# Four graph layers on one core: the identity of pass 3 added into the adjacency tiles, and the normalization's scale and bias made on GpSimd

## What is computed

```python
h = relu(layernorm(x)); x = x + (D_r^-1 A) h W_in + (D_c^-1 A^T) h W_out
h = relu(layernorm(x)); x = x + silu(A silu(A h W + b) W + b)
h = relu(layernorm(x)); x = x + relu((A_n h) W + b)        # A_n = s (A + I) s, s = rsqrt(rowsum(A + I))
h = relu(layernorm(x)); x = x + relu(A_n (h W) + b)        # the same A_n
```

## Time and profile before

| | before |
| --- | --- |
| median of 3 runs | 1132.54 us (1132.07 to 1133.21) |
| profiled execution | 1133.05 us |
| its span, first to last instruction | 1131.3 us |
| TensorE, busy share of the span | 98% |
| VectorE | 93% |
| ScalarE | 81% |
| GpSimd | 4% |
| granted TensorE clock | 0.999 (2.4 GHz) |
| HBM | 360 GB/s over the span |

### The profile page before, as it was taken

How to read it: one execution, slowest core, us unless ns; L and a number is a source line. 1 busy time by engine, 2 the same in 40 slices (tenths; PEclk the granted TensorE clock), 3 DMA queues, 4 the chain that set the end, 5 groups by cost and what they waited for, 6 DMA issues and landing times.

```text
span 1131.3 us, 14740 instructions
## 1 busy us (share of the span) xinstructions
PE 1107.9 (98%) x5056; PEld 912.8 (81%) x5056; DVE 1049.6 (93%) x1452; ACT 912.9 (81%) x1278; POOL 48.0 (4%) x40
## 2 busy tenths in 40 slices
PE   5999999999999999999999999999999999999998
PEld 4778888888888778888888888888888888788886
DVE  6899997999999999898988999999999999998987
ACT  6999987799788578788887888888778778877774
POOL 0000000000000000000000111112111121100000
PEclk9999999999999999999999999999999999999999
DMA  9999998999998899999999999999999999999992
GB/s 328 404 391 393 405 409 313 341 393 409 371 377 315 308 381 375 409 371 360 376 373 383 332 371 364 345 374 340 393 348 347 368 361 335 337 410 370 380 365 113
DMA packets 113835, 408.36 MB, mean 361 GB/s; under 512 B 12640, under 2 KB 13920, under 8 KB 113760
## 3 DMA queue, kind: packets, MB, share of 16 engines
q1 hardware_dynamic: 113760, 407.42, 95.3%
HBM read 405.27 MB, written 2.10 MB: 360 GB/s over the span
## 4 chain that ended last, share of the span: by engine, by line
PE 72%; DVE 17%; ACT 3%; issue 3%; DMA 3%; SPq 1%; ACTq 0%; DVEq 0%
PE bank L701 45%; PE bank L705 23%; DVE a_lo L485 11%; PE bank L722 3%; DMA raw<-in_adj_t_dram 2%; ACT a_hi L357 1%; DVE x_sb L580 1%; ACT a_hi L359 1%; DMA raw<-in_adj_dram 1%; DVE stats L516 1%; DVE acc L573 1%; DVE h_lo L485 1%; SPq L299 1%; DVE h_lo L509 1%; PE bank L763 0%
## 5 line engine op out<-in xcount | busy, mean ns | idle before, releaser
L485 DVE TENSOR_TENSOR a_lo<-raw,a_hi 128x1024 fp32r<-128x1024 f32 x560 | 659.2, 1218 | 40.7 <-ACT a_hi L357 21.9
L701 PE MATMUL bank<-a_hi,h_hi 128*128 128x512 f32 x1400 | 437.2, 393 | 12.1 <-DVE h_lo L509 10.3
L705 PE MATMUL bank<-a_lo,h_hi 128*128 128x512 f32 x1400 | 434.9, 392 | 5.6 <-DVE a_lo L485 4.8
L357 ACT ACTIVATE a_hi<-raw 128x1024 fp32r<-128x1024 f32 x368 | 376.9, 1055 | 71.0 <-PE bank L705 55.6
L701 PE MATMUL bank<-a_hi,h_lo 128*128 128x512 f32 x1400 | 432.0, 390 | 0.0
L705 PEld LDWEIGHTS bank<-a_lo,h_hi 128*128 128x128 f32 x1400 | 260.8, 188 | 70.0 <-DVE a_lo L485 17.1
L701 PEld LDWEIGHTS bank<-a_hi,h_hi 128*128 128x128 f32 x1400 | 259.1, 188 | 65.1 <-DVE h_lo L509 10.2
L701 PEld LDWEIGHTS bank<-a_hi,h_lo 128*128 128x128 f32 x1400 | 263.1, 188 | 55.6
L359 ACT ACTIVATE a_hi<-raw 128x1024 fp32r<-128x1024 f32 x192 | 201.8, 1054 | 27.0 <-PE bank L705 12.7
L485 DVE TENSOR_TENSOR a_lo<-acc,a_hi 128x1024 fp32r<-128x1024 f32 x144 | 170.5, 1219 | 14.3 <-ACT a_hi L357 11.6
L357 ACT ACTIVATE a_hi<-acc 128x1024 fp32r<-128x1024 f32 x144 | 148.4, 1055 | 24.9 <-PE bank L705 23.8
(11 more groups left out here) (75 smaller groups left out, 420.8 us busy)
## 6 DMA issues: line engine op xcount, KB each, us to landing
raw<-in_adj_t_dram SPq DMA_DIRECT2D x496, 512.0 KB, 6.7
acc<-in_adj_t_dram SPq DMA_DIRECT2D x144, 512.0 KB, 6.5
raw<-in_adj_dram SPq DMA_DIRECT2D x128, 512.0 KB, 7.0
out_dram<-x_sb SPq DMA_DIRECT2D x7, 256.0 KB, 6.7
x_sb<-in_x_dram SPq DMA_DIRECT2D x3, 512.0 KB, 11.8
x_sb<-in_x_dram SPq DMA_DIRECT2D x2, 256.0 KB, 4.1
out_dram<-x_sb SPq DMA_DIRECT2D x2, 128.0 KB, 1.7
w_sb<-in_L_gnn_W_dram SPq DMA_DIRECT2D x3, 64.0 KB, 10.3
```

The lines of the kernel that those rows point to most:

```text
L357: act.activation(sub_hi_of(n), sub_raw(n), ACT.Copy).then_inc(sub_hi, 1)
L485: dve.tensor_tensor(sub_lo_of(n), sub_raw(n), sub_hi_of(n).bitcast(F32), ALU.subtract).then_inc(sub_lo, 1)
L701: pe.matmul(bank[half][:, :], weights, hi_a[:, half * GW:(half + 1) * GW], start=start and weights is hi_w, stop=False)
L705: last = pe.matmul(bank[half][:, :], hi_w, lo_a[:, half * GW:(half + 1) * GW], start=False, stop=stop)
```

## The change

1. `identity_product` goes, with its rounded identity. `plus` runs for pass 3 as well as for pass 4, so VectorE makes 32 more adds of 128 x 128. `PLUS_AHEAD` is 5 instead of 2.
2. For the normalizations made in passes 2 and 3 the five operations of VectorE in `ln_affine` go. GpSimd does the same arithmetic in seven operations behind its two, each waiting for the one in front except the second. `ln_stats` waits, before it overwrites the statistics, for the bias of the half before.
3. Moved: `LATER` 16 to 13; in pass 2 the silu at 6 instead of 7; the statistics at 7 instead of 8; scale, bias and ReLU with the rounding at 17 instead of 13; `h_lo` at 18 instead of 14.

```diff
-        PLUS_AHEAD = 2
+        PLUS_AHEAD = 5
-        for g in range(NG):
-            for b in range(CB):
-                n = n_of(SWEEPS, g, g * CB + b)
-                plus_n[n] = len(plus_cols)
-                plus_cols[n] = slice(b * P, (b + 1) * P)
+        for sweep in (3, 4):
+            for g in range(NG):
+                for b in range(CB):
+                    n = n_of(sweep, g, g * CB + b)
+                    plus_n[n] = len(plus_cols)
+                    plus_cols[n] = slice(b * P, (b + 1) * P)
...
-        LATER, LATER_FIRST = 16, 8
+        LATER, LATER_FIRST = 13, 8
-        AT_SILU = {1: 8, 2: 7}
-        AT_STATS = 8
-        AT_AFFINE = 11
-        AT_HI = {1: 8, 2: 13, 3: 13}
-        AT_LO = {1: 9, 2: 14, 3: 14}
-        AT_OWN = 20
+        AT_SILU = {1: 8, 2: 6}
+        AT_STATS = 7
+        AT_HI = {1: 8, 2: 17, 3: 17}
+        AT_LO = {1: 9, 2: 18, 3: 18}
...
+                    pool.wait_ge(rstd_ready, n + 1)
+                    pool.tensor_tensor(newton[:, 0, :], rstd[:, :], rstd[:, :], ALU.mult).then_inc(newton_done, 1)
+                    pool.tensor_tensor(newton[:, 1, :], rstd[:, :], d_isqrt[:, GB * q:GB * q + GB], ALU.mult)\
+                        .then_inc(newton_done, 1)
+                    pool.wait_ge(newton_done, m + 2)
+                    pool.tensor_tensor(newton[:, 0, :], newton[:, 0, :], std[:, :], ALU.mult).then_inc(newton_done, 1)
+                    pool.wait_ge(newton_done, m + 3)
+                    pool.tensor_scalar(newton[:, 2, :], newton[:, 0, :], -0.5, 1.5, ALU.mult, ALU.add)\
+                        .then_inc(newton_done, 1)
+                    pool.wait_ge(newton_done, m + 4)
+                    pool.wait_ge(act_ready, split_n(sweep, q))
+                    pool.tensor_tensor(lnscale[:, :], newton[:, 2, :], newton[:, 1, :], ALU.mult).then_inc(lnscale_ready, 1)
+                    pool.wait_ge(lnscale_ready, n + 1)
+                    pool.tensor_tensor(std[:, :], mv[:, :, 0], lnscale[:, :], ALU.mult).then_inc(minus_ready, 1)
+                    pool.wait_ge(minus_ready, n - LN_BEFORE[2] + 1)
+                    pool.tensor_scalar(lnbias[:, :], std[:, :], -1.0, None, ALU.mult).then_inc(lnbias_ready, 1)
...
                 dve.wait_ge(stats_ready, n + 1)
+                if n > NQ:
+                    dve.wait_ge(lnbias_ready, n)
...
-                            for half in late(AT_AFFINE, g, s):
-                                ln_affine(ps, 2 * pg + half)
...
-                        if sweep == 3 and s == AT_OWN:
-                            identity_product(sweep, g, bank)
```

## The result

The changed kernel takes **1148.72 us** (median of six runs, 1145.68 to 1151.95), the kernel before 1132.30 (six runs, 1131.17 to 1133.21). The ratio is 1.0143, with a 95% interval of 1.0127 to 1.0160. The forecast was 1126 us, its range 1122 to 1142: sign and range both missed. The six runs lie in two clusters, three from 1145.7 to 1147.1 and three from 1150.4 to 1152.0; the profiled execution belongs to the upper one (1151.95 us, span 1150.2).

The account below looks back on a forecast made before the run. TensorE and, where its lead is gone, VectorE's round with the chain were taken to set the time. 11.0 us go and 4.5 come, -6.5 from the median 1132.54: 1126 us, range 1122 to 1142.

Parts of the forecast that it names:

- C: Time from GpSimd's first operation to the bias in each half of passes 2 and 3; forecast 9.0 us.
- I let both go at the end of the third subtract: GpSimd's first two new operations, without a wait between them, both pass 3.3 us in; five more follow, one a subtract.
- Rival 2: GpSimd's second new operation needs a subtract of its own: C = 10.2, +6.5 us, 1139 us; chance 0.27.
- rival 1: GpSimd's operations are short, C at most 7.8; about 1.2 us stay as dips, 1122.7 us; chance 0.17.
- TensorE's round and the identity products, 11.0 us to be had: Passes 2 and 3 into pass 4: four identity products (7.4 us) and 3.6 us of waits go.
- Identity adds at no cost of their own: 32 more adds on VectorE in pass 3, 6.5 us in all, 1.6 a group, costed at zero.
- Nothing waits up to C = 7.8; near C = 9.5 about 1.2 us for each 0.1 us of C: GpSimd's chain in passes 2 and 3: hidden up to 7.8 us; at 9.5 gain and loss sum to zero.
- dips: Inside a group, residual, statistics and `h_lo` lie closer: a 3.6 us dip in VectorE's thin lead; 3 us allowed.
- One operation per subtract, with its end 0.06 us behind: A GpSimd operation reading SBUF gets its data when VectorE's subtract in flight is through: one per 1.135 us.
- I: Time of the ten VectorE subtracts around GpSimd's chain: C + 3.5 us, at least 11.35; forecast 12.5.
- Rival 3: Every GpSimd operation takes the add's 1.17 us whatever VectorE does: C = 11.2, +21, 1153.6 us; chance 0.10.
- rival 4: GpSimd's reads hold up VectorE's subtracts: at 0.1 us for each of 144 operations, 14 us at risk; chance 0.04.

Follow-up runs that it names:

- experiment 3: The changed kernel with the identity added behind the subtract of a substep instead of ahead of it: 1141.34 us, ratio 1.0077.
- experiments 1 and 5: 1: changed kernel with scale and bias made by VectorE again, 1127.17 us; 5: experiment 3's kernel without the Newton step's four GpSimd operations, 1122.75 us.
- experiment 2: The changed kernel with TensorE's identity product kept in pass 3, adds in pass 4 only, two ahead: 1140.00 us, ratio 1.0065.
- experiment 4: Experiment 3's kernel without GpSimd's product of 1/std with the inverse square root of the degree, eight operations instead of nine: 1128.67 us, ratio 0.9966.
- the 128x256 case: The kernel before with a two-input 128x256 VectorE add behind the statistics of passes 2 and 3: 1135.70 us, one run.

## Why the prediction was wrong

**The step that failed** is the one on C. The prediction said of the two new operations without a wait between them: "I let both go at the end of the third subtract". One did (0.21 us), the other was issued into the next subtract and took 1.18. C is 10.2 instead of 9.0, and the forecast was wrong from 9.5 on, as it said itself. The text had the reason for this in its second rival (a read behind another finds the next subtract running) and had taken it for the less likely on the strength that nothing waits between the two. That says when an operation may be issued, not when its data come. The pace is one operation a subtract over the whole chain (nine in 10.20 us, 1.13 each), with or without a wait, and the prediction had put nine into eight. This step alone turns the sign: with it and without the long waits the kernel takes 1141.3 us (experiment 3), a loss, though still inside the range.

**The step that was missing.** Nothing in the prediction has GpSimd kept out for ten subtracts. It went by 16 equal durations of 1082 to 1089 ns, which all stood in one situation: a subtract directly behind the statistics. The change itself altered that situation in two halves of pass 3, by putting an add there, and whether it is the add or the subtract that follows the statistics could be seen from the order of the instructions. That the price of this would be 11.9 us could not be seen from any row of before. It is the long waits that put the time outside the range.

Point by point:

- *TensorE's round and the identity products, 11.0 us to be had*: held. With C out of the way the kernel takes 1122.75 us, 9.5 less than before and what rival 1 had to the tenth.
- *Identity adds at no cost of their own*: held in sum in experiments 1 and 5, apart from the long waits that an add in the wrong place makes. Experiment 3 beside experiment 2 shows the other side: with C at 10.2 taking the products off TensorE gained nothing (1141.3 and 1140.0). I put that down to VectorE's round setting the time there and not TensorE.
- *Nothing waits up to C = 7.8; near C = 9.5 about 1.2 us for each 0.1 us of C*: the second held. Measured: 5.66 us gives 1122.8, 9.07 gives 1128.7, 10.2 gives 1141.3. From 9.07 to 10.2 that is 12.7 us for 1.13, so 1.1 us for each 0.1. The 7.8 lies between two of these points and was not tried. At 9.0 the prediction had 1126.0, at 10.2 it had 1139.0: each 2 to 3 us low, the first with 3 us allowed for dips and the second with none. A part of this can be read off the traces: the prediction took one C for every half, but where identity adds stand between the subtracts the chain's pace is 1.34 us, and C reaches 11.2 us in experiment 3 and 10.5 in experiment 4; in experiment 2, without adds in pass 3, no half but the first is over 10.2. What each half's excess costs in time, no run shows.
- *One operation per subtract, with its end 0.06 us behind*: held wherever a subtract was in flight. The Trainium skill's rule (SBUF — State Buffer, section Who interferes with whom: a VectorE instruction with two SBUF inputs and a GpSimd instruction that reads SBUF contend, and the later waits fully for the other) agrees with the trace in these halves, and in the 128x256 case, where GpSimd's operation ended at 670.31, 0.06 us behind the small operation of VectorE (669.86 + 0.39). In the long halves the trace goes beyond it: GpSimd waited for up to ten subtracts of VectorE and the adds between them, not for one instruction.
- *Rival 2* was the mechanism and, without the long waits, the size: 13.69 us for I, 10.2 for C, 1141.3 us against 1139. The measured 1148.7 is that plus 7.4 us for one or two long waits.
- *Rival 3* falls (0.20 to 0.21 us with VectorE idle or a subtract ending), and *rival 4* too: VectorE's subtracts keep their pace beside the chain, nine in 10.31 us (647.60), steps of 1.14.
- *What the profile after would show*: ScalarE's wait for the bias over 2 us where C is above 10 (3.14 us above; of these halves only the first, with 1.84 us, is under 2), TensorE's wait for `a_lo` at 15 us or more (20.0). Both were named as rival 2's marks.

The difference, put together: +9.0 us from C = 10.2 with adds and schedule in (experiment 3 against the kernel before, 1141.3 - 1132.3), and +7.4 from the long waits (1148.7 - 1141.3), which makes the 16.4 measured.

**What stays open** is why GpSimd, asking between 0.1 us behind and 0.02 us ahead of the start of a subtract, gets in after one subtract in some halves and is kept out until VectorE stops in others whose rows read the same, and why this strikes the first operation of a chain and none of the later ones. For first operations the window is shown by the table, its cause isn't. Nor was it tried whether a gap of VectorE shorter than its wait for GpSimd or for a tile would let the operation through.

## What to carry to other kernels

Price a small operation that is moved to GpSimd beside a stream of VectorE's SBUF operations by the number of those that must end before it does, one for each GpSimd operation, with or without a semaphore between them; count the operations of the chain, for a single one can decide the sign. Then look at what stands directly behind the instruction that releases GpSimd: keep the long operation there (a 128x1024 subtract, or here the 128x512 `h_lo`) and put the short one behind it. And when all measured durations of an operation agree, ask whether they were all taken in the same situation, and whether the change leaves it so.

## What the runs showed of the hardware

- A GpSimd operation on 128x4 takes 0.19 to 0.23 us with VectorE idle, the power 1.01 to 1.04. Beside 128x1024 subtracts of 1.22 us, one a subtract gets through, and most take 1.04 to 1.18 us (1.24 to 1.28 with an identity add between the subtracts).
- GpSimd's operation can be kept waiting for as long as VectorE runs without a pause: 11.91 and 13.53 us for an addition of 4 elements a partition. It happened to the first operation of a chain in 32 of 56 halves in which a subtract began between 0.11 us before and 0.02 us behind GpSimd's start, and in none of 168 in which it began 0.16 to 0.17 us before or 0.14 us and more behind. It happened to none of 106 later operations that started in the same window.
- A useless VectorE operation of 0.14 us (128x16) behind the statistics made a kernel of 1132 us slower by 12.7 us, one of 0.39 us in the same place by 3.6 (a single run each).
